# A perceiver block on one core: x3t copied in halves, one query copy on VectorE, a maximum between two sums

## What is computed

```python
# 1 cross attention: 16 heads, latent width 32, queries from the normed x, keys and values from ctx
C_q, C_kv = ln(x) @ Wq_d, ctx @ Wkv_d
scores = einsum('bnhl,bkl->bhnk', (C_q @ W_qk).reshape(b, n, 16, 32), C_kv) / sqrt(32)
x = x + einsum('bhnk,bkhd->bnhd', softmax(scores), (C_kv @ Wv_u).reshape(b, k, 16, 32))
# 2 self attention: one head of width 128
q, k, v = split(ln(x) @ Wqkv + bqkv)
x = x + softmax(q @ k.T / sqrt(128)) @ v @ Wo + bo
# 3 ffn: Hadamard transform, 4-bit rows, ternary weight (512 x 512)
xh = ln(x) @ hadamard
scale = max(abs(xh), axis=-1, clip 1e-5) / 7
x = x + (clip(round(xh / scale), -8, 7) * scale) @ ternary(weight).T
```

## Time and profile before

| | |
|---|---|
| median of 3 runs | 325.86 us (325.75 to 326.93) |
| the profiled execution | 325.88 us |
| its span, first to last instruction | 324.1 us |
| outside the span | 1.78 us |
| TensorE busy | 309.0 us (95%) |
| VectorE busy | 239.9 us (74%) |
| ScalarE busy | 211.5 us (65%) |
| GpSimd busy | 88.7 us (27%) |
| granted TensorE clock | 0.999 |

### The profile page before, as it was taken

The page is one execution under the profiler, slowest core; times in us unless marked ns, Lnnn a source line. Parts: engine busy times, 40 slices in busy tenths (PEclk is TensorE's granted clock), DMA queues, the critical chain, the costliest instruction groups (busy, mean ns, idle before and its releaser), DMA issues.

```text
span 324.1 us, 8470 instructions
## 1 busy us (share of the span) xinstructions
PE 309.0 (95%) x3157; PEld 218.6 (67%) x3172; DVE 239.9 (74%) x517; ACT 211.5 (65%) x581; POOL 88.7 (27%) x129
## 2 busy tenths in 40 slices
PE   8987999999999999999999999999999999999995
PEld 6765766767576867667576857666675767575754
DVE  1599458886888678886879678886888778886335
ACT  1485877767585777767686877766776868682310
POOL 2000634140323224240333224240414123232220
PEclk9999999999999999999999999999999999999999
DMA  7992402050301403050302302050302010000000
GB/s 219 292 385 66 146 3 97 2 188 10 129 3 50 148 3 128 0 193 1 129 0 93 101 32 97 0 194 0 129 2 69 0 67 1 34 3 32 0 34 32
DMA packets 13482, 25.25 MB, mean 78 GB/s; under 512 B 3217, under 2 KB 3985, under 8 KB 13457
## 3 DMA queue, kind: packets, MB, share of 16 engines
q1 hardware_dynamic: 13456, 24.91, 23.0%
HBM read 20.71 MB, written 4.19 MB: 77 GB/s over the span
## 4 chain that ended last, share of the span: by engine, by line
PE 66%; DVE 18%; ACT 5%; issue 3%; DMA 3%; SPq 2%; POOL 1%; DVEq 0%; POOLq 0%
PE ps L684 14%; PE ps L722 6%; PE ps L632 6%; PE ps L799 5%; PE ps L831 4%; PE ps L642 4%; PE ps L822 4%; DVE sum_a L459 4%; PE ps L779 3%; PE ps L726 3%; DMA w_rows<-weight 3%; DVE mx L450 3%; PE ps L734 2%; PE ps L649 2%; PE ps L805 2%
## 5 line engine op out<-in xcount | busy, mean ns | idle before, releaser
L320 ACT ACTIVATE prob<-ps,nmx,qk_scale 128x128 f32<-128x128 f32 x256 | 96.1, 466 | 41.3 <-DVE nmx L454 41.3
L684 PE MATMUL ps<-had_s,x3t 128*128 128x512 f32 x128 | 59.2, 605 | 2.9 <-ACT x3t L314 2.7
L450 DVE TENSOR_REDUCE mx<-ps 128x8 f32<-128x1024 f32 x32 | 39.0, 1218 | 16.3 <-PE ps L799 16.3
L684 PEld LDWEIGHTS ps<-had_s,x3t 128*128 128x128 f32 x128 | 23.0, 189 | 32.3 <-issue 28.4
L459 DVE TENSOR_REDUCE sum_a<-prob 128x8 f32<-128x1024 f32 x32 | 37.5, 1210 | 2.4 <-ACT prob L320 2.4
L303 POOL TENSOR_TENSOR qk_scale<-aux,power 128x1 f32<-128x1 f32 x16 | 8.8, 550 | 98.6 <-DVE aux L534 98.6
L314 ACT ACTIVATE prob_t<-ps 128x512 f32<-128x512 f32 x64 | 35.2, 622 | 0.5
L632 PE MATMUL ps<-ident,prob 128*128 128x128 f32 x256 | 33.7, 275 | 0.6 <-ACT prob L320 0.6
L307 POOL TENSOR_TENSOR res<-prod,x 128x512 f32<-128x512 f32 x15 | 19.1, 1277 | 54.4 <-DVE prod L567 54.4
L722 PE MATMUL ps<-x2t,wqkv_s 128*128 128x128 f32 x256 | 32.6, 281 | 0.4 <-ACT x2t L314 0.4
L722 PEld LDWEIGHTS ps<-x2t,wqkv_s 128*128 128x128 f32 x256 | 29.8, 191 | 1.9 <-ACT x2t L314 1.0
(11 more groups left out here) (119 smaller groups left out, 543.7 us busy)
## 6 DMA issues: line engine op xcount, KB each, us to landing
ct<-ctx_cols SPq DMA_DIRECT2D x16, 512.0 KB, 4.7
xt<-x_cols SPq DMA_DIRECT2D x16, 256.0 KB, 2.7
xr<-x_rows SPq DMA_DIRECT2D x16, 256.0 KB, 4.2
y<-res SPq DMA_DIRECT2D x15, 256.0 KB, 2.0
w_rows<-weight SPq DMA_DIRECT2D x1, 1024.0 KB, 8.3
had_s<-hadamard SPq DMA_DIRECT2D x1, 1024.0 KB, 8.4
wqkv_s<-wqkv SPq DMA_DIRECT2D x1, 768.0 KB, 10.0
wqk<-w_qk SPq DMA_DIRECT2D x2, 128.0 KB, 4.4
```

The source lines that it names most:

```text
L320: last = nc.scalar.activation(prob[:, h, :], ps[:, h // 4, (h % 4) * P:(h % 4) * P + P], ACT.Exp, bias=nmx[:, h:h + 1], scale=qk_scale[:])
L450: V.tensor_reduce(mx[:, h], ps[:, 2 * half:2 * half + 2, :].rearrange("p r (c k) -> p (r c) k", c=EC), AX.X, ALU.max).then_inc(done["mx"], 1)
L684: mm = pe.matmul(ps[:, B4, :], x3t[:, c, :], had_s[:, c, :], start=(c == 0), stop=(c == EC - 1))
```

## The change

It has three parts. ScalarE copies `x3t` in two halves of two chunks each, each half with its own count of `read["x3t"]`, and L684 waits for the first half ahead of its first matmul and for the second ahead of its third. In the long rounds the copy of bank 1 to `q_t[:, 1]` goes from ScalarE to VectorE, where it stands between the sums and `mx2`. In the short rounds VectorE takes `mx2` and `nmx2` between the two halves of the sums.

```diff
--- before.py
+++ after.py
@@ -334,7 +334,9 @@
                 if quant:
                     after(act, made["x3t"], i - 2)
                     after(act, made["had"], i - 3)
-                    copy(x3t[:], ps[:, B3, :].rearrange("p (c t) -> p c t", c=EC)).then_inc(read["x3t"], 1)
+                    for h in range(2):
+                        copy(x3t[:, 2 * h:2 * h + 2], ps[:, B3, 2 * h * P:(2 * h + 2) * P].rearrange("p (c t) -> p c t", c=2))\
+                            .then_inc(read["x3t"], 1)
                 if cross:
                     exps(6, 8).then_inc(done["exp"], 1)
                 if front:
@@ -372,8 +374,6 @@
                 if front and alone(i):
                     after(act, made["qt"], i + 1)
                     q_copy(1 - par, query_bank(i))
-                elif front and par == 1:
-                    q_copy(1, 1)
                 if self_:
                     after(act, done["nmx2"], i - 1)
                     after(act, done["rsum2"], i - 2)
@@ -512,12 +512,18 @@
                 if cross:
                     after(dve, done["rsum"], i - 1)
                     sums(0)
-                    sums(1)
+                    if par == 1:
+                        sums(1)
+                if front and par == 1 and not alone(i):
+                    dve.wait_ge(made["qt"], k + 3)
+                    V.tensor_copy(q_t[:, 1], ps[:, 1, :].rearrange("p (c b q) -> p b c q", c=EC, b=2)).then_inc(read["qt"], 1)
                 if self_:
                     after(dve, made["s2"], i - 1)
                     V.tensor_reduce(mx2[:], ps[:, B3, 0:SQ], AX.X, ALU.max).then_inc(done["mx2"], 1)
                     after(dve, done["mx2"], i - 1)
                     V.tensor_scalar(nmx2[:], mx2[:], -float(D2) ** -0.5, None, ALU.mult).then_inc(done["nmx2"], 1)
+                if cross and par == 0:
+                    sums(1)
                 if quant:
                     after(dve, made["qit"], i - 2)
                     V.tensor_scalar(qi_t[:], qit_bank.rearrange("p (c t) -> p c t", c=EC), QMIN, None, ALU.max)\
@@ -675,12 +681,13 @@
                 if quant:
                     if first and i >= PAIRS:
                         keep_busy(2, 0)
-                    after(pe, read["x3t"], i - 2)
                     after(pe, read["int"], i - 3)
                     if first and i == 2:
                         pe.wait_ge(row_read, 1)
                         pe.wait_ge(had_ready, EC)
                     for c in range(EC):
+                        if c % 2 == 0:
+                            pe.wait_ge(read["x3t"], (i - 2) * 2 + 1 + c // 2)
                         mm = pe.matmul(ps[:, B4, :], x3t[:, c, :], had_s[:, c, :], start=(c == 0), stop=(c == EC - 1))
                     mm.then_inc(made["had"], 1)
                 if self_:
```

## The result

Over 16 runs of each, the changed kernel takes 323.93 us (323.19 to 326.22) and the kernel before 326.62 (325.59 to 328.82): a ratio of 0.9922, 95% interval 0.9905 to 0.9938, 0.8% less. The profiled execution of the changed kernel took 324.15 us. In its profile many lines have other numbers: L642 is now L648, L649 L655, L684 L691, L691 L698, L722 L729, L752 L759, L779 L786, L786 L793 and L799 L806; `mx2` is L522, `qi_t` L529, `prod` L573 and `x3` L580.

A forecast was written before the change was run, and what follows sets the result against it. TensorE's list was taken to bound the kernel, with three places where it waits for a copy. From 325.88 us, parts 1, 2 and 3 take 0.66 + 0.60 + 1.11 = 2.37, giving 323.5 us; range 322.3 to 325.3.

The forecast's parts named there:

- what is late next takes it all: Loop's short rounds: L684 starts 0.22 to 0.27 earlier, but exponentials hold the `x2t` copy, so L722 stays: gain 0.
- the 0.22 of the three rounds without that chain: Rounds 2, 16 and 17: no exponentials hold `x2t`, so the half copy's 0.22 passes in each, 0.66 in all.
- L684 does pull L722: Rival, loop's short rounds: exponentials come earlier than thought, so 0.27 of four rounds passes, 322.4 us; chance 0.12.
- the rival of the costly halves: `x3t` copies, rounds 2 to 17: 0.16 extra on the path in each of 16, 326.1 us; chance 0.04.
- The rival that L799's spacing is TensorE's own: Long rounds, L786 to L799: one more semaphore wait keeps 0.37, so 0.60 is missing, 324.1 us; chance 0.11.
- the 0.28 more in round 4: Round 4, ahead of L786: TensorE idles 0.28 more because VectorE is later, so part 3 was given 0.45 there.
- that sign: Short rounds: if L450 starts over 1.25 behind L799, part 3's gain is gone.
- The rival that this list decides the short rounds: Short rounds, before L450: VectorE's list 0.2 longer than added up leaves nothing of 1.11, 324.6 us; chance 0.14.
- The slower rival (a late sum): Moved sum delays L450, `x3` and next L649 in seven rounds; slower from 0.34 each, 327.0 us at 0.5; chance 0.07.
- the 0.16 that the prediction allowed: ScalarE, `x3t` halves: two copies of 0.38 against one of 0.60, 0.16 more work, taken to lie in idle time.

The follow-up runs named there:

- e7_x2t_earlier: Changed kernel with the wait for the first `x3t` half written first and, in short rounds, `x2t` copied after two late exponentials, not three: 322.80 us, ratio 0.9866.
- e10_x2t_whole: e7_x2t_earlier with `x3t` copied whole by one instruction again: 324.58 us, ratio 0.9944 to the kernel before.
- e4_wait_order: Changed kernel with the two waits ahead of L691 swapped, the one for the first `x3t` half written first: 324.44 us, ratio 0.9929 to the kernel before.
- part 2's 1.33: Kernel before with only the long rounds' second query copy moved to VectorE: 1.33 us shorter from round 2 on; 325.65 us, ratio 0.9969.
- e3_max_between: Kernel before with only `mx2` and `nmx2` put between the two sums in short rounds: 325.67 us, ratio 0.9968.
- e5_two_ops: Kernel before with one spare tiny VectorE copy in each of rounds 1 and 3: one run of 324.99 us against 326.73 for the kernel before.
- e6_sum_twice: Changed kernel with a spare, unread VectorE sum ahead of the moved second sum in each short round: one run of 331.80 us.
- e9_six_ops: Kernel before with three spare small VectorE copies in each of rounds 1 and 3: one run of 327.80 us.

## Why the prediction was right, and where it was not

323.5 was predicted, 323.93 measured; the range held it. The prediction counted from 325.88, while the kernel before took 326.62 over the 16 runs: the gain was 2.69, 2.37 were predicted. From round 2 on the profiles give 2.41. That this is so near is luck in part: part 1 gave 0.06 less, part 3 0.19 more, round 15 took 0.08 back, and the standstill, which was not foreseen, was in the price of part 3.

**The bound.** TensorE's list with three places where it stands for a copy: right. In the loop's short rounds of the changed profile the wait of L691 is gone, L806 follows L793 in both kinds of round, and L729 still follows the copy of `x2t` (161.24 + 0.60 = 161.84, then 161.90).

**Part 1: 0.60 measured, 0.66 predicted.** The step "what is late next takes it all" was right for the loop: L691 stands before L729 by 5.19 as predicted (5.1), and e7_x2t_earlier and e10_x2t_whole show both sides of it. It was wrong for rounds 12 and 14, which gained 0.07 each where 0 was put: there the copy of `x2t` waited as much for the transpose of `x2n` as for the exponentials. The kernel before, round 12:

```profile
232.44 1.16 ACT L320 ACTIVATE prob<-ps,nmx,qk_scale 128x128 f32<-128x128 f32 x3 [2.14 <-DVE nmx L454]
232.92 0.60 PE L691 MATMUL ps<-ident,x2n 128*128 128x128 f32 x4
...
233.56 0.60 ACT L314 ACTIVATE x2t<-ps 128x512 f32<-128x512 f32 x1
```

L691 is here the transpose of `x2n` (L698 in the changed kernel), from which the copy of `x2t` is made. The copy starts 0.04 behind the end of L691 (233.52), and 1.12 behind the start of the exponentials where it is 1.04 in the loop. With the halves L691 ends earlier and the exponentials are what holds it, so a part of the gain passes. The two were nearly tied, and I took the loop's order of them for these rounds too. The mis-sized term is the 0.22 of the three rounds without that chain: round 2 gave 0.16 and the last two 0.30 and not 0.44. The first half is there 0.22 earlier as worked out, but the wait for it moved from the weight load to an instruction ahead of it, and that costs 0.09 each time, of which 0.03 comes back within the group (e4_wait_order). With its order changed and `x2t` in time, the term measures 0.21 to 0.22 a round (e10_x2t_whole). The rival "L684 does pull L722" fell, though e7_x2t_earlier makes it true by moving one exponential behind the copy; the rival of the costly halves fell too.

**Part 2: 0.59 measured in the six long rounds, 0.60 predicted.** The copy takes 0.69 (0.7 was taken). The Trainium skill, "VectorE: DVE Perf Modes", section on the TRN2 errata, gives an estimate of 0.66; the trace is 0.03 above it. The rival that L799's spacing is TensorE's own fell: 0.37 became 0.25. What the prediction missed is that two more instructions on VectorE move a standstill that stood on the path in the loop's short rounds. Alone that is worth 0.37 + 3 x 0.14 = 0.79 of part 2's 1.33. In round 15 the reverse happens: in the kernels with the query copy on VectorE, the sums start 0.44 behind `qi` where it was 0.34, and the round is 0.08 longer.

**Part 3: 1.30 measured in the loop's short rounds, 1.11 predicted.** 0.50 and 3 x 0.27 (0.26 in round 10) against 0.45 and 3 x 0.22; rounds 2, 12 and 14 gave nothing of their own, as said (e3_max_between). Part 3 also hides the standstill, since the maximum now waits for L759 by 0.68 whether the sums come a little later or not; that is why parts 2 and 3 together give no more in these rounds than part 3 alone. e3_max_between shows it: from `floor` to the step it still has 0.46 in round 4 and 0.21 to 0.23 in rounds 6 to 10, and its rounds are as short as those of the changed kernel. It also says what the 1.30 is made of. Against e5_two_ops, where the standstill costs nothing, the maximum between the sums gives 0.12 in round 4 and 0.13 in the others, 0.51 in all; the other 0.79 is the standstill. The rows that the prediction summed up had it in them, so the sum came out, but what was read as the sums' lateness (the 0.28 more in round 4 above all) was largely this. L450 starts 1.30 behind L806 without idle time. The prediction had said that over 1.25 part 3 would be gone, and it was not: that sign was too strict, because `x3` has 0.26 of room (e6_sum_twice). The rival that this list decides the short rounds fell. The slower rival (a late sum) did not happen, and its threshold was too low: in e6_sum_twice 1.13 of lateness made a round 0.87 longer, so the first 0.26 was free.

**The total against the runs.** The difference of medians is 2.69 us, the profiles from round 2 on give 2.41; the difference is within the interval (0.5 us to either side), and the filling of the pipeline varies by more.

## What to carry to other kernels

When a wait goes, follow the chain that starts elsewhere: the half copy was worth nothing while the next copy stood behind exponentials, and 0.20 a round once one of them was moved behind it. So look for the pair of edits, not for each alone, and see which instruction carries the wait that ends last: written ahead of those that are long fulfilled, it came to sit on the weight load, where it cost least. When two edits of one round each gain alone, expect the sum only if they remove different waits; judge them by equal rounds of the steady state, since the filling of a pipeline varies by more than such edits bring.

## What the runs showed of the hardware

- VectorE can stand still for 0.13 to 0.37 at a fixed place of its instruction stream with no wait that explains it, in the loop and in the rounds behind it, and two or six added instructions far ahead move that place (in round 4, 0.46, 0.09 and 0.10 from `floor` to the step in the kernel before, e5_two_ops and e9_six_ops). The cause is open. An edit may gain or lose that much for no reason of its own; in a kernel where VectorE is waited for, a spare instruction is a cheap trial.
- A semaphore wait that ends last costs TensorE about 0.09 more when it stands on an instruction of its own ahead of the matmuls than when it stands on their weight load (0.53 against 0.44 from the start of the half copy to the matmuls in rounds 16 and 17, 0.55 against 0.46 in round 2).
- Two copies of 256 columns back to back take ScalarE 0.66 against 0.60 for one of 512: the 0.38 of each overlap by 0.10, so the split cost 0.06 and not the 0.16 that the prediction allowed.
- At the start of two of the twelve executions TensorE's granted clock fell to 1.2 GHz (0.54 and 0.50 from 30 to 32 us), and these had the longest starts, 50.4 and 49.6 against 46.7 to 48.9.
